# A transformer layer pair on eight cores: token-major residual, background stages behind both attentions

## The chip, the cores and the metric

The kernel runs on the 8 cores of one Trainium2 chip, in two dies of four cores. Every core computes one of the 8 batch elements alone; the cores exchange nothing. The metric is the device time of the slowest core, in microseconds (us).

## The reference, cut to what matters

One batch element is 2048 tokens of 1024 features. In sequence:

```python
x = x + attn_a(layernorm(x))   # 8 heads; two 64-wide halves q1,q2 / k1,k2 of each 128-wide head
x = x + ffn(layernorm(x))
x = x + attn_b(layernorm(x))   # 16 heads of 64, rotary, causal softmax
x = x + ffn(layernorm(x))      # the same ffn weights again
attn_a: # for each head, over all 2048 keys:
L1, L2 = cos_scale * l2norm(q1) @ l2norm(k1).T, cos_scale * l2norm(q2) @ l2norm(k2).T
G = tanh(delta_gain * (L1 - L2))
y = (softmax(L1 + G) - lambda * softmax(L2 - G)) @ v      # then an RMS norm over 128, @ Wo.T + bo
ffn: y = x @ int4_rounded(kernel) + bias + (x @ a) @ b    (a is 1024 x 16)
```

## The kernel before, in words

The residual stream is kept feature-major: `resid[c]` holds 128 features of all 2048 tokens (f32), eight such tiles. All stages follow one another, with a barrier of all engines (`phase_barrier`) between most of them:

1. Preparation: load the input, small constants; quantize the ffn weights on VectorE and ScalarE, 8 row blocks one after another, and store them in DRAM (`d_wqb`).
2. `emit_ln`: sums over features by matmuls with a column of ones (`ln_px`, `ln_pxq`), row arithmetic on one partition, a broadcast by matmul (`ln_bc`), two VectorE passes for each tile.
3. Attention A in two halves of four heads (`hg`). `run_qk_proj` makes Q and K; each group of 128 features and 512 tokens takes 8 matmuls, is squared, summed by head half with two one-column matmuls, and the norm goes through one-partition rows (`qrows`) with Ln and Exp on ScalarE. `emit_proj_tm` makes V.
4. The attention loop has 256 steps for each half, 512 in all; a step is 128 keys by 512 queries for both softmaxes. TensorE: a pair of logits (`a_pL<-aQ,aK`, each on 64 rows of the array), the scaled difference (`a_pD`), two additions of G by an identity and a negative identity (`id_bf`, `idn_bf`), two value products (`a_pY`) and two one-column sums (`a_ps`). ScalarE: one Tanh (`a_G<-a_pD`) and one Exp of 1024 columns (`a_E<-a_pL`). There are two buffers of each, and the order of an engine's instructions is written out by hand. The sums are turned into reciprocals by way of DRAM (`scr`, `xpf`, `scrb`, `a_rb`).
5. Output projection into `resid`, `emit_ln`, `emit_ffn`.
6. Layer norm, rotary tables, then two halves of attention B: projections with a swap matmul (`b_pswap`) and three VectorE passes for the rotation, then 160 steps of 128 keys by up to 512 queries for two heads: Exp (`b_E`), three value or sum matmuls, a mask on diagonal blocks.
7. Output projection, layer norm, ffn, and the store of all of `resid`.

Each instruction is recorded by a helper, so every row of the profile names line L119; the tile names tell them apart.

## Time and profile before

| | |
|---|---|
| median of 3 runs | 6092.5 us (6050.47 to 6096.83) |
| profiled execution, slowest core | span of 6033.8 us from first to last instruction |
| TensorE / VectorE / ScalarE / GpSimd busy | 2880.8 / 1456.7 / 1464.2 / 319.3 us |
| mean granted TensorE clock, die 0 / die 1 | 0.727 / 0.718 of full |
| moved by DMA | 83.52 MB, mean 14 GB/s |

The span is that of one profiled execution; the timed runs are 17 to 63 us above it. Busy time of TensorE counts the modelled time in the array, and matmuls overlap each other.

### The profile page before, as it was taken

How to read it: one execution, taken by the hardware profiler on the slowest of the kernel's cores; microseconds unless marked ns; L12 is line 12 of the kernel's file. 1: busy time of each engine (PE TensorE's matmuls, PEld its weight loads, DVE VectorE, ACT ScalarE, POOL GpSimd, SP SyncE). 2: the span in 40 equal slices, each digit the busy share in tenths (PEclk: the TensorE clock that was granted, in tenths of full speed). 3: DMA queues.
4: the chain of work that ended last, by engine and by line, in shares of the span. 5: the costliest groups of instructions: out<-in, count | busy, mean ns of one | idle time of the engine just before them, and what ended most of it. 6: DMA issues, size and time to landing. Idle time of an engine off the chain costs nothing.

```text
span 6033.8 us, 35983 instructions; the slowest of 8 cores (5950.4 to 6033.8 us)
## 1 busy us (share of the span) xinstructions
PE 2880.8 (48%) x9536; PEld 759.7 (13%) x9536; DVE 1456.7 (24%) x2432; ACT 1464.2 (24%) x1528; POOL 319.3 (5%) x535
## 2 busy tenths in 40 slices
PE   0012436666555443466556654352446544655625
PEld 0000111111111011111111111110111111111201
DVE  1335330000111133200100111515431225222241
ACT  0000113444444311144444441000003320233000
POOL 0100000000000000000000000000001100011000
PEclk9985556677777756777877686686776667766858
DMA  2000000000000000000000001000100000000101
GB/s 87 8 9 11 11 18 3 6 6 6 6 8 6 7 13 14 14 6 6 6 6 7 6 6 27 6 13 2 40 17 5 6 15 23 12 6 5 30 3 68
DMA packets 107520, 83.52 MB, mean 14 GB/s; under 512 B 45086, under 2 KB 94750, under 8 KB 105022
## 3 DMA queue, kind: packets, MB, share of 16 engines
q1 hardware_dynamic: 79710, 55.07, 3.0%
q0 software_dynamic: 27616, 26.14, 2.3%
q8 instruction: 87, 1.43, 0.1%
q14 instruction: 107, 0.88, 0.1%
HBM read 70.08 MB, written 10.98 MB: 13 GB/s over the span
## 4 chain that ended last, share of the span: by engine, by line
PE 34%; DVE 19%; DMA 19%; ACT 14%; issue 11%; DVEq 1%; ACTq 0%; POOLq 0%; SPq 0%; PEldq 0%; POOL 0%
ACT a_E L119 8%; PE pj_p L119 7%; PE a_pY L119 6%; PE a_pL L119 5%; DMA scrb<-xpb 4%; PE a_pD L119 3%; PE a_ps L119 3%; PE f_p L119 3%; DMA b_rb<-scrb 3%; DMA scr<-rr 3%; DVE tmpf L119 3%; PE tm_pv L119 2%; ACT qrows L119 2%; DMA wqb<-qout 2%; DMA xpf<-scr 2%
## 5 line engine op out<-in xcount | busy, mean ns | idle before, releaser
L119 PE MATMUL a_pY<-a_E,aV 128*128 128x512 bf16 x1024 | 393.0, 474 | 811.7 <-ACT a_E L119 811.6
L119 ACT ACTIVATE a_G<-a_pD,gvec 128x512 bf16<-128x512 f32 x512 | 352.7, 689 | 1197.2 <-PE a_pD L119 1188.7
L119 ACT ACTIVATE a_E<-a_pL,ccol 128x1024 bf16<-128x1024 f32 x512 | 569.6, 1112 | 94.0 <-PE a_pL L119 90.8
L119 ACT ACTIVATE b_E<-b_pS,ccol 128x1024 bf16<-128x1024 f32 (+1 forms) x320 | 312.3, 987 | 1121.3 <-PE b_pS L119 1119.3
L119 PE MATMUL b_pYa<-b_E,bV 128*65 128x512 bf16 (+1 forms) x320 | 145.0, 453 | 366.5 <-DVE b_E L119 262.4
L119 PE MATMUL ln_px<-ln_xb,ones_col 128*1 128x512 bf16 x128 | 74.4, 581 | 468.6 <-DVEq L119 468.6
L119 POOL DMA_DIRECT2D scr<-rr x160 | 81.3, 508 | 4023.2 <-DVEq L119 3914.5
L119 PE MATMUL a_pD<-aQ,aKn 128*128 128x512 bf16 x512 | 253.6, 495 | 44.4 <-DVEq L119 23.5
L119 ACT ACTIVATE qrows<-qrows 1x4096 bf16<-1x4096 bf16 x32 | 115.7, 3617 | 588.6 <-DVEq L119 587.1
L119 PE MATMUL a_pL<-a_G,id_bf 128*128 128x512 bf16 x512 | 257.9, 504 | 0.0
L119 PE MATMUL a_pL<-a_G,idn_bf 128*128 128x512 bf16 x512 | 253.7, 495 | 0.0
L119 PE MATMUL a_pL<-aQ,aK 64*128 64x512 bf16 x1024 | 252.0, 489 | 2.9 <-DVEq L119 2.9
L119 DVE COPY a_Yr<-a_pY 128x512 f32<-128x512 f32 x64 | 41.2, 686 | 862.0 <-PE a_ps L119 862.0
L119 PE MATMUL a_ps<-a_E,ones_col 128*1 128x512 bf16 x1024 | 242.8, 470 | 0.0
L119 PE MATMUL pj_p<-xnA,pj_wb 128*128 128x512 bf16 x512 | 203.0, 568 | 73.9 <-DVE pj_wb L119 73.9
L119 ACT ACT_TABLE_LOAD x69 | 88.5, 1283 | 540.4 <-DVEq L119 329.5
L119 PE MATMUL pj_p<-bxn,pj_wb 128*128 128x512 bf16 x512 | 154.4, 456 | 121.4 <-DVE pj_wb L119 121.4
L119 PEld LDWEIGHTS a_pY<-a_E,aV 128*128 128x128 bf16 x1024 | 67.2, 99 | 1143.9 <-issue 1143.9
L119 PE MATMUL f_p<-fxn,f_wqb 128*128 128x512 bf16 x512 | 149.5, 445 | 110.7 <-DVEq L119 57.1
L119 DVE RECIPROCAL xpb<-xpf 128x8 bf16<-128x8 f32 x96 | 18.7, 195 | 746.0 <-DMA xpf<-scr 484.4
L119 PE MATMUL pbcq<-qrows,ones_row 1*64 1x512 bf16 x128 | 40.5, 615 | 251.8 <-DVEq L119 251.8
L119 PE MATMUL b_pYb<-b_E,bV 128*64 128x512 bf16 (+1 forms) x320 | 150.1, 469 | 0.0
(151 smaller groups left out, 3170.0 us busy)
## 6 DMA issues: line engine op xcount, KB each, us to landing
a_rb<-scrb POOLq DMA_DIRECT2D x32, 256.0 KB, 3.9
pj_wf<-WqkT SPq DMA_DIRECT2D x32, 256.0 KB
out<-resid SPq DMA_DIRECT2D x8, 1024.0 KB, 10.2
resid<-xT SPq DMA_DIRECT2D x4, 1024.0 KB, 11.9
resid<-xT POOLq DMA_DIRECT2D x4, 1024.0 KB, 12.5
pj_wf<-WqT SPq DMA_DIRECT2D x16, 256.0 KB
pj_wf<-WkT SPq DMA_DIRECT2D x16, 256.0 KB
tm_wvhf<-WvT SPq DMA_DIRECT2D x16, 256.0 KB
```

Of the source, the lines that this page charges most:

```text
L119: r = getattr(eng, name)(*args, **kw)
```

## The change

The kernel is rewritten. In words, with the names of the new code:

- The residual is token-major: a block `b` is 128 tokens by 1024 features, 16 blocks, four of them at a time in `x`. Layer norm statistics come from `bn_stats` and `bn_aggr` on VectorE, the power -0.5 from GpSimd, and one VectorE pass applies them. Between the ffn and attention B the residual goes to DRAM (`d_x2`) and the normalized tokens too (`d_xn3`).
- The features are brought onto partitions by transposing DMAs on SyncE's queue (`Slot.turn`): of normalized blocks (`turn_ln1`, `turn_ln`, `load_xs`) and of attention outputs (`turn`, `turn_b`). Blocks 0 to 7 of the first layer norm are turned by 8 matmuls each with an identity (`turn_pe`), evicted by ScalarE and VectorE.
- Phase 1 makes Q, K and V of all heads: 64 groups for Q and K (8 matmuls and one with a block matrix `blk` that sums squares over a head half on all partitions; Square, Ln and Exp of 512 columns on ScalarE; one VectorE pass) and 32 for V. The weights are cast to bf16 by GpSimd's DMAs. The quantization (`quantize`) is a generator stepped between the groups and in phase 2; the result `wq` stays in SBUF.
- Phase 2 is attention A in 64 units (256 queries and one head) of 8 steps, 512 steps in all; a step is 256 keys by 256 queries. E is the stationary operand and V, with a column of ones, the moving one, so that outputs are token-major and the sums come with them: 8 matmuls of 129 columns. G is added on VectorE (`step_S`), on odd steps for the lower half by one matmul with a negative identity (`step_A`). The per-unit normalization is on GpSimd (`y_out`, `y_rms`).
- After 8 units a generator `after_a` does output projection, layer norm, ffn and the next layer norm of two blocks; `Background.step` puts up to 1.6 (later 3) matmuls of 512 columns of it into each attention step.
- Phase 3 makes K, V and Q of attention B for all heads (96 groups; GpSimd does the last addition of the rotation), phase 4 is attention B in 320 steps, with E stationary again (65 columns) and `after_b` in the background. The last four blocks' `after_b` runs after the loop.

The core of the diff (removed lines are those of the listing above):

```diff
+class Background:
...
+    def step(self, rate, cap):
+        self.clock += 1
+        due = [c for c in self.calls if c[0] <= self.clock]
+        self.calls = [c for c in self.calls if c[0] > self.clock]
+        for _, fn in due:
+            fn()
+        self.credit = min(self.credit + rate, cap)
+        while self.gens and self.credit > 0:
+            cost = next(self.gens[0], None)
+            if cost is None:
+                self.gens.popleft()
+                return
+            if cost <= 0:
+                return
+            self.credit -= cost
+    def drain(self):
...
+    def turn_pe(n):
+        for _ in range(n):
+            b, a_tok = late_turn.popleft()
+            t, tb = b // 4, b % 4
+            toks = []
+            pe.wait(a_tok)
+            for k, q in enumerate((ac, ve)):
+                pe.wait(pT_free[k])
+                for c in range(4):
+                    col = 128 * (4 * k + c)
+                    mm(pe, pT[k][:, 128 * c:128 * (c + 1)], wq[:, b % 8, col:col + 128],
+                       ident[:, :], True, True)
+                q.wait(pe.done())
+                out = xn[t % 2][:, 4 * k:4 * k + 4, 128 * tb:128 * (tb + 1)]
+                if q is ac:
+                    act(ac, out, blocks_of(pT[k][:, :], 4), AF.Copy)
+                else:
+                    copy(ve, out, blocks_of(pT[k][:, :], 4))
+                pT_free[k] = q.done()
...
+        ac.wait(p_tok, sq_free[i])
+        act(ac, sqb[i][:, :], bank[:, :], AF.Square)
+        sq_tok = ac.done()
+        def rest():
+            pe.wait(sq_tok, pss_free[i])
+            mm(pe, pss[i][:, :], blk[:, :], sqb[i][:, :], True, True)
+            s_tok = pe.done()
+            sq_free[i] = s_tok
+            ac.wait(s_tok, rn_free[i])
+            act(ac, rn[i][:, :], pss[i][:, :], AF.Ln, bias=lntiny)
+            pss_free[i] = ac.done()
+            ac.wait(pss_free[i])
+            if is_q:
+                act(ac, rn[i][:, :], rn[i][:, :], AF.Exp, scale=-0.5, bias=lnc[:, h:h + 1])
+            else:
+                act(ac, rn[i][:, :], rn[i][:, :], AF.Exp, scale=-0.5)
+            ve.wait(ac.done())
+            cap = c1e6[:, h:h + 1] if is_q else 1.0 / COS_EPS
+            stt(ve, dst[:, h, QT * t:QT * (t + 1)], rn[i][:, :], cap, bank[:, :], OP.min, OP.mult)
+            rn_free[i] = pqk_free[bi] = ve.done()
+        late.append(rest)
...
+        for t in (t0, t1):
+            for h in range(HA):
+                group_qk(Q, W3[0], w_tok[0:2], t, True, h)
+                if pair == 0 and t == t0:
+                    if h < 4:
+                        ln1_stats(4 + h)
+                    if 1 <= h < 5:
+                        ln1_apply(3 + h)
+                    if h >= 4:
+                        turn_pe(1)
+                if pair == 1:
+                    next(quant, None)
+        for t in (t0, t1):
+            for h in range(HA):
+                group_qk(K, W3[1], w_tok[2:4], t, False, h)
+                if pair == 0:
+                    (ln1_stats, ln1_apply)[h % 2](8 + 4 * (t - t0) + h // 2)
+                if pair == 1:
+                    next(quant, None)
+                if (pair == 0 and t == t1) or (pair == 1 and h % 2 == 1):
+                    next_v()
+        while todo_v:
+            next_v()
+    phase_barrier()
+    p1.close()
+    s1.close()
...
+        pe.wait(w_tok, *y_toks)
+        for hf in range(2):
+            cols = slice(512 * hf, 512 * (hf + 1))
+            bank = state["banks"].take(pe)
+            for c in range(NCH):
+                mm(pe, bank[0], Q[:, c, tok], Wo[:, c, cols], c == 0, c == NCH - 1 and not bias)
+                yield 1
+            if bias:
+                pe.wait(state["row97"])
+                mm(pe, bank[0], sel[:, :], fbb[:, cols], False, True)
+            p_tok = pe.done()
+            yield 0
+            ve.wait(p_tok, x_tok[b])
+            tt(ve, x[:, b % 4, cols], bank[0], x[:, b % 4, cols], OP.add)
+            bank[1] = ve.done()
+            yield 0
+            ve.wait(bank[1])
+            ln_stats(b, hf)
...
+        for hf in range(2):
+            cols = slice(512 * hf, 512 * (hf + 1))
+            bank = state["banks"].take(pe)
+            for c in range(NCH):
+                mm(pe, bank[0], xt[:, c, :], wq[:, c, cols], c == 0, False)
+                yield 1
+            pe.wait(l_tok)
+            mm(pe, bank[0], lora[k][:, :], fbb[:, cols], False, True)
+            p_tok = pe.done()
+            yield 0
+            ve.wait(p_tok)
+            stt(ve, x[:, b % 4, cols], bank[0], qscale[:, 0:1], x[:, b % 4, cols],
+                OP.mult, OP.add)
+            bank[1] = x_tok = ve.done()
+            yield 0
...
+    def after_a(n, y_toks):
+        last = n == NTB // 2 - 1
+        q = ve
+        two = (2 * n, 2 * n + 1)
+        if not last:
+            load_x(di["xN"], 2 * n + 2)
+            load_x(di["xN"], 2 * n + 3)
+        for i, b in enumerate(two):
+            yield from out_proj(b, y_toks, state["Wo"], True)
+            layer_norm(b, q, i, lambda a_tok, b=b, i=i: turn_ln(b, i, a_tok, b % 4))
+        if last:
+            state["last_o"](pe.done())
+        for i, b in enumerate(two):
+            yield from ffn(b, b % 4)
+            sy.wait(state["x"])
+            x2_tok[b] = r_st.next(sy).start(sy, rows_of(d_x2, b), x[:, b % 4, :])
+            layer_norm(b, q, 2 + i, lambda a_tok, b=b, i=i: keep(b, 2 + i, a_tok))
+        while xn3_tok[two[1]] is None:
+            yield 0
...
+    def on_pe(s):
+        return s % 2 == 1
+    def step_L(s):
+        if not 0 <= s < NS:
+            return
+        h, qsl = q_range(s // NKS)
+        pe.wait(S_tok.get(s - 2), P_tok.get(s - 2))
+        for jj in range(2):
+            j = 2 * (s % NKS) + jj
+            js = slice(128 * j, 128 * (j + 1))
+            cs = slice(QA * jj, QA * (jj + 1))
+            mm(pe, pL[2 * (s % 2)][:, cs], K[0:64, h, js], Q[0:64, h, qsl], True, True, (0, 0))
+            if on_pe(s):
+                pe.add(lambda e, s=s, cs=cs, js=js, h=h, qsl=qsl, jj=jj: e.matmul(
+                    pL[2 * (s % 2) + 1][:, cs], K[64:128, h, js], Q[64:128, h, qsl],
+                    start=jj == 0, stop=False, tile_position=(64, 0), skip_group_check=True))
+            else:
+                mm(pe, pL[2 * (s % 2) + 1][:, cs], K[64:128, h, js], Q[64:128, h, qsl], True, True,
+                   (64, 0))
+        L_tok[s] = pe.done()
+    def step_A(s):
+        if not 0 <= s < NS or not on_pe(s):
+            return
+        pe.wait(G_tok[s])
+        mm_in(pe, pL[2 * (s % 2) + 1][:, :], nident[:, :], Gt[s % G_RING][:, :], False, True)
+        A_tok[s] = pe.done()
+    def step_D(s):
+        if not 0 <= s < NS:
+            return
+        u = s // NKS
+        h, _ = q_range(u)
+        pe.wait(G_tok.get(s - 1), qn_tok[u])
+        for jj in range(2):
+            j = 2 * (s % NKS) + jj
+            mm(pe, pD[:, QA * jj:QA * (jj + 1)], K[:, h, 128 * j:128 * (j + 1)], Qn[u % 2][:, :],
+               True, True)
+        D_tok[s] = pe.done()
+    def step_tanh(s):
+        if not 0 <= s < NS:
+            return
+        ac.wait(D_tok[s], S_tok.get(s - G_RING), A_tok.get(s - G_RING))
+        act(ac, Gt[s % G_RING][:, :], pD[:, :], AF.Tanh)
+        G_tok[s] = ac.done()
+    def step_S(s):
+        if not 0 <= s < NS:
+            return
+        ve.wait(L_tok[s], G_tok[s], E_tok.get(s - S_RING))
+        sx, gt = Sx[s % S_RING], Gt[s % G_RING]
+        tt(ve, sx[:, 0, :], pL[2 * (s % 2)][:, :], gt[:, :], OP.add)
+        if not on_pe(s):
+            tt(ve, sx[:, 1, :], pL[2 * (s % 2) + 1][:, :], gt[:, :], OP.subtract)
+        S_tok[s] = ve.done()
+    def step_exp(s):
+        if not 0 <= s < NS:
+            return
+        e = E[s % E_RING]
+        ac.wait(Y_tok.get(s - E_RING))
+        if on_pe(s):
+            ac.wait(A_tok[s])
+            act(ac, e[:, 1, :, :], pL[2 * (s % 2) + 1][:, :], AF.Exp)
+            P_tok[s] = ac.done()
+            ac.wait(S_tok[s])
+            act(ac, e[:, 0, :, :], Sx[s % S_RING][:, 0, :], AF.Exp)
+        else:
+            ac.wait(S_tok[s])
+            act(ac, e[:, :, :, :], Sx[s % S_RING][:, :, :], AF.Exp)
+        E_tok[s] = ac.done()
+    def step_Y(s):
+        if not 0 <= s < NS:
+            return
+        u, k = s // NKS, s % NKS
+        h, _ = q_range(u)
+        pe.wait(E_tok[s])
+        if k == 0:
+            pe.wait(y_evac.get(u - 1))
+        for jj in range(2):
+            for sg in range(2):
+                for b in range(2):
+                    mm_in(pe, pY[sg][:, VA * b:VA * (b + 1)],
+                          E[s % E_RING][:, sg, jj, 128 * b:128 * (b + 1)],
+                       V[:, 2 * k + jj, VA * h:VA * (h + 1)],
+                       k == 0 and jj == 0 and b == 0, k == NKS - 1 and jj == 1)
+        Y_tok[s] = pe.done()
...
+    for s in range(-3, NS + NKS):
+        step_tanh(s + 2)
+        step_exp(s)
+        u, k = (s - NKS) // NKS, s % NKS
+        if u < 0 or k == 0 or k >= 3:
+            step_Y(s - 1)
+        elif k == 2:
+            step_Y(s - 2)
+            step_Y(s - 1)
+        step_D(s + 3)
+        step_L(s + 2)
+        step_A(s + 1)
+        if u >= 0 and k == 1:
+            y_out(u, 1)
+        step_S(s + 1)
+        if s >= 0:
+            bg.step(1.6, 2.6)
+        if u >= 0:
+            if k == 0:
+                y_out(u, 0)
+            if k == 4:
+                y_rms(u)
+            if k == 6:
+                turn(u)
+        if s >= 0 and k == 5:
+            make_qn(s // NKS + 2)
...
+    def load_xs(t, *free):
+        sy.wait(*xn3_tok[4 * t:4 * t + 4], *free)
+        xs_tok[t] = r_turn.next(sy).turn(sy, xs[t], rows_of(d_xn3, t, QT))
...
+        ac.wait(p_tok, qb_free[i])
+        act(ac, qb[i][:, :], bank[:, :], AF.Copy)
+        b_tok = ac.done()
+        def rest():
+            pe.wait(b_tok, pss_free[i])
+            mm(pe, pss[i][:, :], perm[:, :], qb[i][:, :], True, True)
+            qb_free[i] = pe.done()
+            ve.wait(b_tok, t_free[i], cs_tok[t])
+            tt(ve, t1[i][:, :], bank[:, :], x[:, t, 0:QT], OP.mult)
+            pqk_free[bi] = ve.done()
+            ve.wait(qb_free[i])
+            tt(ve, t2[i][:, :], pss[i][:, :], x[:, t, QT:2 * QT], OP.mult)
+            pss_free[i] = ve.done()
+            po.wait(pss_free[i])
+            tt(po, dst[:, h, sl], t1[i][:, :], t2[i][:, :], OP.add)
+            t_free[i] = po.done()
...
+    def after_b(t, y_toks):
+        four = range(4 * t, 4 * t + 4)
+        for b in four:
+            yield from out_proj(b, y_toks, wo_tok, False)
+            layer_norm(b, ve, b % 4, lambda a_tok, b=b: turn_ln(b, b % 4, a_tok, b % 4))
+        for b in four:
+            yield from ffn(b, b % 4)
+            sy.wait(state["x"])
+            out_tok[b] = x_free[b % 4] = r_st.next(sy).start(sy, rows_of(d_out, b), x[:, b % 4, :])
+            if b + 4 < NTB:
+                load_x(d_x2, b + 4)
...
+        pe.wait(E_tok.get(s - 2))
+        mm(pe, pS[s % 2][:, 0, q0:QT], K[0:64, c, js], Q[0:64, c, qsl], True, True, (0, 0))
+        mm(pe, pS[s % 2][:, 1, q0:QT], K[64:128, c, js], Q[64:128, c, qsl], True, True, (64, 0))
+        S_tok[s] = pe.done()
...
+    for s in range(-2, NB + 5):
+        stepb_exp(s)
+        stepb_Y(s - 2)
+        if 0 <= s - 2 < NB:
+            t, c, j = blocks[s - 2]
+            if j == 4 * t + 3:
+                i = t * (HB // 2) + c
+                k = norm_b(t, c, i, s - 2)
+                turn_b(t, c, i, k)
+        if s >= 0:
+            bg.step(3, 3)
+        stepb_S(s + 2)
+    for k in range(4):
+        state["banks"].add(pS[k // 2][:, k % 2, :], E_tok[NB - 1])
+    bg.drain()
```

## Rows read from the trace of the kernel before

**Rows 1.** Cores: span and mean granted clock, slowest core and both dies.
```profile
core 7: 6033.8 us, clock 0.718
die 0 (median of its cores): 5976.8 us, clock 0.727
```

**Rows 2.** Windows by stage: us, busy (count) of each engine, clock, DMA.
```profile
0.00:380.00 380.00, 0.00 (x0) 0.00 (x0) 98.36 (x154) 20.09 (x21) 44.90 (x87) 1.00 0.13 39
380.00:922.00 542.00, 204.58 (x584) 61.06 (x584) 223.57 (x300) 64.56 (x25) 0.00 (x0) 0.58 0.04 12
922.00:2040.00 1118.00, 683.45 (x2255) 141.47 (x2256) 107.56 (x194) 483.16 (x545) 78.49 (x135) 0.73 0.03 6
2040.00:2540.00 500.00, 194.25 (x621) 58.45 (x621) 154.00 (x210) 81.75 (x43) 5.23 (x9) 0.62 0.05 14
2540.00:3700.00 1160.00, 664.75 (x2276) 141.17 (x2276) 114.76 (x207) 484.84 (x550) 83.16 (x143) 0.75 0.05 6
3700.00:4478.00 778.00, 334.50 (x1138) 116.36 (x1138) 331.31 (x497) 12.10 (x17) 0.54 (x1) 0.73 0.07 20
4478.00:5630.00 1152.00, 610.00 (x2016) 175.99 (x2016) 294.02 (x680) 312.31 (x320) 107.02 (x160) 0.67 0.04 10
5630.00:6034.00 404.00, 189.26 (x648) 65.21 (x648) 133.15 (x190) 5.41 (x8) 0.00 (x0) 0.74 0.11 36
```

**Rows 3.** Chain that ended last, one step of attention A: start, us, what.
```profile
1499.91 0.59 PE a_pY L119 x2
1500.50 0.31 PE a_ps L119 x2
1500.81 0.32 PE a_pL L119 x2
...
1501.61 0.33 ACT a_G L119
...
1502.19 1.12 ACT a_E L119
...
1503.44 0.59 PE a_pY L119 x2
```

**Rows 4.** Costliest groups: shapes, count, busy, mean ns, idle before.
```profile
L119 ACT ACTIVATE a_E<-a_pL,ccol 128x1024 bf16<-128x1024 f32 x512 | 569.6, 1112 | 94.0 <-PE a_pL L119 90.8
L119 ACT ACTIVATE a_G<-a_pD,gvec 128x512 bf16<-128x512 f32 x512 | 352.7, 689 | 1197.2 <-PE a_pD L119 1188.7 <-PE a_pL L119 8.5
L119 PEld LDWEIGHTS a_pY<-a_E,aV 128*128 128x128 bf16 x1024 | 67.2, 99 | 1143.9 <-issue 1143.9
L119 DVE SCALAR_TENSOR_TENSOR resid<-f_p,fb_col,resid 128x512 f32<-128x512 f32 x64 | 48.0, 751 | 233.9 <-PE f_p L119 233.9
L119 DVE TENSOR_TENSOR aQ<-aQ,pbcq 128x512 bf16<-128x512 bf16 x32 | 22.0, 688 | 35.2 <-PE pbcq L119 35.2
```

**Rows 5.** Timeline of ScalarE: two Exp of 1024 columns back to back.
```profile
4495.88 2.15 ACT L119 ACTIVATE b_E<-b_pS,ccol 128x1024 bf16<-128x1024 f32 x2 [0.85 <-PE b_pS L119]
```

**Rows 6.** Timeline of weight loads in a dense run of 512-column matmuls.
```profile
3751.35 4.63 PEld L119 LDWEIGHTS pj_p<-aQ,pj_wb 128*128 128x128 bf16 x22 [0.20 <-issue]
```

**Rows 7.** Window of core 7 in its first dense V projection.
```profile
900.00:910.00 10.00, 10.00 (x40) 4.15 (x39) 3.46 (x5) 0.00 (x0) 0.00 (x0) 0.81 0.00 0
```

**Rows 8.** The same window on core 0.
```profile
900.00:910.00 10.00, 10.00 (x48) 4.55 (x47) 4.15 (x6) 0.00 (x0) 0.00 (x0) 1.00 0.01 2
```

**Rows 9.** Timeline of core 7's weight loads there, first and thirty-second.
```profile
900.24 0.11 PEld L119 LDWEIGHTS tm_pv<-tm_wvh,xnA 128*128 128x128 bf16 x1 [0.15 <-issue]
...
908.38 0.11 PEld L119 LDWEIGHTS tm_pv<-tm_wvh,xnA 128*128 128x128 bf16 x1 [0.15 <-issue]
```

**Rows 10.** DMA queue: packets, MB, share; issues: count, KB, us to landing.
```profile
q1 hardware_dynamic: 79710, 55.07, 3.0%
...
a_rb<-scrb POOLq DMA_DIRECT2D x32, 256.0 KB, 3.9
...
out<-resid SPq DMA_DIRECT2D x8, 1024.0 KB, 10.2
```

2008 lines of the change are left out of this document (857 added, 1151 removed).

## The prediction

> **What bounds the kernel now.** I read the cores first: the slowest spans 6033.8 us, the other die's median is within 1% of it, so one core tells the story [rows 1]. Then windows cut by stage [rows 2]. The reader should see that no engine is full anywhere: in attention A (1118 + 1160 us) TensorE is busy 61% and 57% and ScalarE 43% and 42%; outside the attentions ScalarE does almost nothing and TensorE 25 to 45%; in the first 380 us TensorE does nothing at all. The stages stand in a row, so the kernel is bound by waits, and each stage's latency counts in full. The chain of waits shows the same inside a step of attention A [rows 3]: value products, sums, logits, then Tanh, then Exp, then the next value products, 1503.44 - 1499.91 = 3.53 us a step where it runs at its best, of which ScalarE works 1.8 and TensorE about 2. Over the halves it is (1118 + 1160)/512 = 4.45 us, since the idle lets the granted clock drop to 0.73 [rows 2].
>
> **Prices.** Dense 512-column matmuls start 0.215 us apart at a granted clock of 1.0 (4.63 us for 22 loads, less one load of 0.11) [rows 6]. In the dense V projection core 7 was granted 0.81 for all of the window, its TensorE busy without a gap [rows 7], and starts were (908.38 - 900.24)/31 = 0.263 us apart [rows 9]; core 0 kept 1.00 in the same work [rows 8]. A pair on 64 rows each runs together, 0.32 us for both [rows 3]. Exp of 1024 columns takes 1.11 us, back to back 2.15 - 1.11 = 1.04 [rows 4, 5]; Tanh of 512 takes 0.69, and Exp starts 0.58 after it [rows 3, 4]. VectorE takes 0.69 for 512 columns with a PSUM input, 0.75 with three operands [rows 4]. No row has a 129- or 65-column matmul that loads new weights each time. Below, it cannot beat a quarter of 0.215, 0.054; above, a whole weight load of 0.099 [rows 4] that nothing hides. I take 0.075, since loads are pulled ahead of the running matmul in every dense row, but a 129-column one is too short to hide one fully.
>
> **The clock decides the sum.** The new kernel keeps TensorE dense nearly throughout, on all cores at once. The only stretch here like that is rows 7, and it ran at 0.81 on the slower die. I take 0.81 for TensorE-bound stages. The Trainium skill (TensorE: Matmul & The Clock Gate, Part 1) states that dense matmuls on three or more cores of a die bring that die to 13/16 of the clock for as long as the load lasts. By that rule, the trace agrees on core 7 (0.81) and not on core 0 (1.00); under the rule both dies would drop, and the sum would be the one I take.
>
> **Part by part, removed against added.**
> 1. *Preparation*, 380 us [rows 2]. Quantization moves between projection groups and behind attention A: 24 VectorE passes of 1024 columns plus reductions, hidden because VectorE otherwise has one or two 0.7 us passes in each 2.3 us group; without that cover some 40 us. What stays is filling: four 512 KB token blocks and 2 MB of the first weights (1 MB lands in 10.2 us when eight are in flight [rows 10]), then statistics, GpSimd power, apply and turn. 25 us exposed, bounds 15 and 50.
> 2. *First norm, Q, K, V*, 542 + 500 = 1042 us [rows 2], becomes 64 x 9 + 32 x 8 = 832 matmuls: 832 x 0.263 = 219 us (179 at full clock). ScalarE has Square, Ln, Exp in each Q or K group: 0.58 + 0.69 + 0.58 and about 0.2 of waits (Exp waits for its own engine's Ln) = 2.05, under TensorE's 9 x 0.263 = 2.37, but over 1.94 at full clock. 222 us; 190 at full clock.
> 3. *Attention A*, 2278 us. TensorE in a step: 8 x 0.075 = 0.60; logits 2 pairs of 256 columns, 0.32; difference 0.22; half an addition 0.11; background 14 blocks x (36 x 0.215 + 0.5) = 115 us / 512 = 0.22. Sum 1.47, or 1.47/0.81 = 1.81. ScalarE: even steps 0.58 + 1.04, odd steps 3 x 0.58, mean 1.68. VectorE: 1.5 passes of 0.69 = 1.03, background and eviction 0.35: 1.4, not last. The engines are in order, and one wait is new: there is one difference bank, so `step_D` stands behind the Tanh of the same iteration, and logits, addition and background are queued behind it. TensorE's iteration is then 0.79 (Tanh and its signal; the value products fit in it) + (0.22 + 0.32 + 0.11 + up to 0.35 background) = 1.8 at full clock and 0.79 + 1.23 = 2.02 at 0.81. Taking 2.05: 512 x 2.05 = 1050 us (1.85: 947). With 0.054 or 0.099 for the small matmul the value products stay between 0.43 and 0.98, so only the upper end reaches past the 0.79: 0.2 x 512 = 100 us more. Plus 15 us to fill, load the identity and a ScalarE table.
> 4. *Output projection, norms, ffn of A*, 340 of the 778 us: behind attention, priced above. Each step's matmuls go between `step_A` and the next value products, so they delay the latter on TensorE; that is the 0.35. Exposed: 5 us at the end, and the last two blocks, in part 5.
> 5. *Projections of B*, the other 438 plus the 260 inside the B window: again 832 matmuls, 219 us (179). In each group ScalarE has one copy, VectorE two passes (1.4), GpSimd one 512-column addition; all under 2.37 if GpSimd's is. Before it 1 MB has to be transposed after the last value product: 12 us [rows 10]. The last two blocks' background, 74 matmuls = 19 us, and its norms, of which 20 stay exposed. 270 us (221).
> 6. *Attention B*, 892 us without the projections. Full steps: TensorE 0.32 + 8 x 0.075 = 0.92, ScalarE 1.04; diagonal ones about 0.6 and 0.75. Without background ScalarE leads: 0.97 on average. Twelve blocks of background are 12 x 12 = 144 steps with three more matmuls: (0.87 + 0.65)/0.81 = 1.85. 32 first steps 27 us, 144 x 1.85 = 266, 144 x 1.08 = 156: 449 us (387). Start-up 10.
> 7. *Output of B*, 404 us: three quarters hidden; the last four blocks are 4 x 36 x 0.263 = 38 us, plus a norm, a transpose and the last store, 20 us. 58 us (50).
>
> Sum: 25 + 222 + 1050 + 15 + 5 + 270 + 459 + 58 = **2104 us** of span, against 6034. The timed runs before are 17 to 63 us over the span, the median 59; that gives a median near **2140 us**. At full clock throughout: 25 + 190 + 947 + 15 + 5 + 221 + 397 + 50 = 1850, median 1890.
>
> **GpSimd and the transposes** have no row of their own. GpSimd gets five 256-column passes and some ten tiny ones in each unit of 8 steps (16 us), and one 512-column pass in each rotation group. Below zero is excluded, as it frees nothing that is last; it costs nothing up to about 2.5 us for a 256-column pass and 2.3 us for the 512-column one. The nearest row, VectorE's 0.69 for 512 [rows 4], leaves a factor of three. I take nothing. The Trainium skill (GPSIMD Engine Reference, 3.1) speaks against this part of the change: it calls GpSimd the wrong place for ordinary elementwise work, about twice VectorE's time; no run here shows it yet, and an estimate from its 4497 ns for 2048 columns is 1.1 to 1.3 us for the rotation's addition, still hidden.
>
> **Rivals.**
> *A: the clock stays at 1.0* on the slowest core as core 0's did [rows 8]: 1890 us. For it: one die shows it. Against it: the slowest core counts, and there are far longer dense stretches. 0.25.
> *B: the in-order chain of attention does not close.* Each engine of a step waits for two others, plus VectorE's background passes ahead of `step_S`. If each step of A loses another 0.4 us and each of B 0.2: 205 + 64 = 270 us, 2400 us. For it: before, a step whose parts sum to about 2 us took 3.53 [rows 3]. Against it: three or four buffers now instead of two, and logits issued two steps ahead. 0.20.
> *C: slower than before, through the transposing DMAs.* They carry 8 blocks of the first norm and 2048 x 1024 elements five more times (outputs of A, second norm, third norm, outputs of B, last norm): 11.5 million 2-byte elements. The hardware queue's packets took 0.030 x 16 x 6033.8 / 79710 = 36 ns each [rows 10]. If a transpose moved each element as a packet, 11.5 million x 36 ns / 16 engines = 26 ms. It decides from 5.4 ns an element, where 11.5 million x 5.4 / 16 makes up the 3900 us gained; that is 5.9 GB/s. Against it: a rewrite of whole blocks needs no such packets, and at the rate of plain copies (1 MB in 10 us) each transpose is hidden. The Trainium skill (DMA: Bandwidth & Descriptors, latency table) gives 261 GB/s for one transposing kernel; no run here shows it. 0.02. A milder form, transposes at a tenth of plain rate, would add some 100 us at the ends of phases and lies in the range.
> *The change does not do what it says*: no time is hidden, as the background waits at the head of its queue. The hidden parts (115 + 100 us of matmuls) would come back, twice with waits: 2350; counted with B.
>
> **How the numbers follow.** Forecast 2140 us, 0.53; A 0.25; B 0.20; C 0.02. The range 1870 to 2430 takes in A with the cheap matmul, and B; the bounds of filling and of the 0.099 matmul lie within. A measurement of this kernel tells about 1% from no change. Faster by over 1%: all but C, 0.975; within 1%: 0.005, a C that lands there; slower 0.02.
>
> **What would show it.** Granted clock 0.81 in the dense phases on core 7 or its like; attention A's period near 2.05 us with ScalarE busy over 85% and the matmuls of `step_D` waiting for Tanh; first matmul of a group before 30 us; B's projections about 2.4 us a group; after the attention B loop some 60 us. The prediction is wrong if the period of A is over 2.4 us, if a transpose takes over 10 us to land, if GpSimd is busy over 80% in attention A, or if the gaps between the phases sum to over 80 us.

## The result, and the profile after

| | before | after |
|---|---|---|
| median | 6067.23 us (6034.74 to 6096.83, 5 runs) | 1807.96 us (1740.35 to 1873.85, 5 runs) |
| span of the profiled execution | [rows 1] | 1738.1 us (time 1740.44) |

The ratio is **0.2868**, 95% interval 0.2848 to 0.2889. Three of the five runs after (1807.96, 1824.82, 1873.85) had the cores of one die or of both at a lower mean clock (0.84 to 0.91 against 0.95 to 0.96), in the same program, so the ratio and every comparison below leave such runs out, while medians and ranges count all runs.

The forecast was 2140 us, range 1870 to 2430. It was wrong: median and profiled execution both lie below the range. The side was that of rival A, the full clock, which was priced at 1890 us; at 1740 us the kernel is 8% below even that.

The slowest core of the changed kernel, span and mean granted clock, answers to [rows 1]; the medians of the two dies are 1734.9 and 1733.3 us, both at 0.957:

```profile
core 2: 1738.1 us, clock 0.957
```

Its stages in windows, columns as in [rows 2]: filling; first norm and projections of A; attention A, cut in four; projections of B; attention B; what is left.

```profile
0.00:34.70 34.70, 4.22 (x33) 3.06 (x34) 11.93 (x28) 4.95 (x6) 12.68 (x22) 1.00 0.87 179
34.70:241.40 206.70, 188.36 (x866) 84.05 (x866) 112.66 (x188) 123.91 (x203) 15.70 (x35) 0.97 0.35 74
...
241.40:450.00 208.60, 186.11 (x1907) 104.99 (x1908) 170.23 (x287) 191.93 (x315) 89.59 (x191) 0.96 0.23 61
450.00:650.00 200.00, 190.82 (x1979) 108.56 (x1978) 162.81 (x285) 191.94 (x313) 95.10 (x217) 1.00 0.13 36
650.00:850.00 200.00, 190.41 (x1980) 108.47 (x1977) 162.12 (x285) 191.35 (x312) 96.29 (x221) 1.00 0.13 38
850.00:1070.00 220.00, 208.86 (x2173) 119.09 (x2172) 179.62 (x313) 211.07 (x343) 104.87 (x240) 1.00 0.14 38
...
1070.30:1326.70 256.40, 203.39 (x927) 90.42 (x926) 98.20 (x157) 57.32 (x96) 96.95 (x98) 0.90 0.32 55
1326.70:1693.40 366.70, 319.17 (x3319) 151.88 (x3320) 127.07 (x360) 296.20 (x320) 16.15 (x51) 0.91 0.28 67
1693.40:1738.00 44.60, 35.13 (x170) 15.25 (x170) 22.20 (x40) 0.00 (x0) 5.85 (x16) 0.92 0.26 74
```

The reader should see two things. In attention A TensorE is busy 95% and ScalarE 96% of each window from 450 us on (89 and 92% in the first), where [rows 2] had 61 and 43% in the first half: two engines are nearly full at once. And the clock column reads 1.00 from 450 to 1070 us, with TensorE busy 95%; the other seven cores show 1.00 there too, at 92 to 95%. The term on which the sum was built, 0.81, is not there. Nor is it in the projections of A, which are the same kind of work as [rows 7]: from 100 to 230 us all eight cores have TensorE busy 98 to 100% at 1.00, here the slowest core:

```profile
100.00:230.00 130.00, 128.27 (x594) 57.62 (x593) 72.44 (x110) 74.43 (x120) 3.96 (x10) 1.00 0.22 56
```

The groups of attention A, columns as in [rows 4]:

```profile
L175 ACT ACTIVATE Gt<-pD 128x512 bf16<-128x512 f32 x512 | 306.5, 599 | 25.4 <-PE pD L164 16.5
L171 PE MATMUL pY<-V,E 128*128 128x129 bf16 x4096 | 308.5, 221 | 11.7 <-ACT E L175 2.6
L164 PE MATMUL pD<-Qn,K 128*128 128x256 bf16 x1024 | 196.2, 273 | 21.0 <-ACT Gt L175 12.7
```

The difference matmuls waited for Tanh (`Gt`) 12.7 us in the whole run, not the better part of every step. Two steps of the loop on TensorE and on ScalarE (start, us, what):

```profile
601.08 0.62 PE L171 MATMUL pY<-V,E 128*128 128x129 bf16 x8
601.53 0.38 PE L164 MATMUL pD<-Qn,K 128*128 128x256 bf16 x2
...
602.17 0.39 PE L164 MATMUL pB<-Wo,Q 128*128 128x512 bf16 x1
602.40 0.62 PE L171 MATMUL pY<-V,E 128*128 128x129 bf16 x8
602.86 0.38 PE L164 MATMUL pD<-Qn,K 128*128 128x256 bf16 x2
603.17 0.39 PE L166 MATMUL pL<-Q,K 64*128 64x256 bf16 x4
603.50 0.39 PE L171 MATMUL pL<-Gt,nident 128*128 128x512 bf16 x1
603.72 0.59 PE L164 MATMUL pB<-Wo,Q 128*128 128x512 bf16 x2
604.15 0.34 PE L171 MATMUL pY<-V,E 128*128 128x129 bf16 x3
```

```profile
601.48 0.63 ACT L175 ACTIVATE E<-Sx 128x512 bf16<-128x512 f32 x1
602.01 0.60 ACT L175 ACTIVATE Gt<-pD 128x512 bf16<-128x512 f32 x1
602.51 1.05 ACT L175 ACTIVATE E<-Sx 128x1024 bf16<-128x1024 f32 x1
603.46 0.59 ACT L175 ACTIVATE Gt<-pD 128x512 bf16<-128x512 f32 x1
603.98 0.60 ACT L175 ACTIVATE E<-pL 128x512 bf16<-128x512 f32 x1
```

TensorE's busy time counts the modelled time in the array, so starts give the better prices. Eight value matmuls take 601.53 - 601.08 = 0.45 us, 0.056 each, though each loads new weights. ScalarE starts something 0.50 to 0.53 us after an operation of 512 columns and 0.95 after one of 1024. An iteration takes 602.40 - 601.08 = 1.32 with one background product (`pB`), 604.15 - 602.40 = 1.75 with an addition and two of them; the mean is 829/512 = 1.62. Between 300 and 1060 us the median from the last difference matmul to the logits is 0.20 us and from the logits to an addition or a background product 0.20 too, against 0.11 between two difference matmuls of the same 256 columns. An estimate from these starts: 0.45 + 0.11 + 0.20 + 0.12 + 0.20, half an addition (0.11) and a background product (0.22) are 1.41 of the 1.62 us, so TensorE is taken for 87% of the loop rather than 95.

At the seam between attention A and the projections of B, and in the first 80 us of the latter, TensorE and SP's queue (start, us, what, idle before):

```profile
1069.95 0.62 PE L171 MATMUL pY<-V,E 128*128 128x129 bf16 x8 [0.38 <-ACT E L175]
1080.95 1.44 PE L164 MATMUL pB<-Wo,Q 128*128 128x512 bf16 x3 [10.38 <-DMA Q<-yt]
1093.00 3.24 PE L164 MATMUL pL<-V,wkb 128*128 128x512 bf16 x8 [10.61 <-DMA V<-xn]
1115.79 3.57 PE L164 MATMUL pL<-V,wkb 128*128 128x512 bf16 x8 [10.48 <-DMA V<-xn]
1150.37 1.01 PE L164 MATMUL pB<-xn,fab 128*16 128x128 bf16 x8 [16.99 <-DMA xn<-xn]
```

```profile
1078.47 1.17 SPq L127 DMA_TRANSPOSE Q<-yt  x1
1079.79 7.63 SPq L127 DMA_TRANSPOSE V<-xn  x1
...
1088.76 23.49 SPq L127 DMA_TRANSPOSE V<-xn  x1
1135.25 2.81 SPq L127 DMA_TRANSPOSE xn<-xn  x1
```

The first K product waits for a 1 MB transpose that stands on the queue behind the last small one, which itself waits for GpSimd's norm of the last rows. The longest of the four waits, 17.0 us, is for a transpose of 256 KB (`xn<-xn`) that the background's last ffn needs: it landed 15.0 us after its issue, with two weight loads of 1 MB (`Wo<-WqB`) under way, where such a transpose takes 3.1 us in the median of the whole run.

### The profile page after: what moved, and what is told of

It reads as the page before. It is cut to its first block, busy times and chain, and to the rows that moved or that the text cites. A ratio compares the mean times of both kernels' runs of the same rounds, so it can differ in the third digit from the quotient of the medians.

```text
span 1738.1 us, 40419 instructions; the slowest of 8 cores (1726.8 to 1738.1 us)
## 1 busy us (share of the span) xinstructions
PE 1526.8 (88%) x13344; PEld 786.1 (45%) x13344; DVE 1046.8 (60%) x1939; ACT 1268.7 (73%) x1904; POOL 533.2 (31%) x1089
## 3 DMA queue, kind: packets, MB, share of 16 engines
q1 hardware_dynamic: 113718, 82.10, 17.8%
q8 instruction: 115, 1.88, 0.4%
## 4 chain that ended last, share of the span: by engine, by line
PE 43%; ACT 22%; issue 11%; DVE 4%; DMA 4%; POOL 1%; SPq 1%; ACTq 0%; DVEq 0%; POOLq 0%
ACT E L175 11%; PE pL L164 9%; PE pY L171 7%; ACT Gt L175 7%; PE pBb L164 6%; PE pB L164 4%; PE pL L166 4%; PE pS L166 4%; PE pYb L171 4%; ACT EB L175 4%; PE pD L164 3%; DMA V<-xn 2%; DVE Sx L184 1%; DMA Q<-ytb 1%; PE pS L164 1%
## 5 line engine op out<-in xcount | busy, mean ns | idle before, releaser
L184 DVE TENSOR_TENSOR Sx<-pL,Gt 128x512 f32<-128x512 f32 x768 | 503.3, 685 | 139.9 <-PE pL L955 53.3
L175 ACT ACTIVATE E<-Sx 128x1024 bf16<-128x1024 f32 (+1 forms) x512 | 433.1, 846 | 16.5 <-DVE Sx L184 16.1
L175 ACT ACTIVATE EB<-pS,cst 128x1024 bf16<-128x1024 f32 (+1 forms) x320 | 296.2, 992 | 73.1 <-PE pS L166 67.5
L175 ACT ACTIVATE Gt<-pD 128x512 bf16<-128x512 f32 x512 | 306.5, 599 | 25.4 <-PE pD L164 16.5
L171 PE MATMUL pY<-V,E 128*128 128x129 bf16 x4096 | 308.5, 221 | 11.7 <-ACT E L175 2.6
L171 PEld LDWEIGHTS pY<-V,E 128*128 128x128 bf16 x4096 | 259.9, 98 | 93.6 <-issue 41.9
L166 PE MATMUL pL<-Q,K 64*128 64x256 bf16 x1536 | 198.7, 274 | 24.0 <-ACT E L175 15.7
L164 PE MATMUL pD<-Qn,K 128*128 128x256 bf16 x1024 | 196.2, 273 | 21.0 <-ACT Gt L175 12.7
L175 ACT ACTIVATE E<-pL 128x512 bf16<-128x512 f32 x256 | 154.1, 602 | 6.0 <-PE pL L171 0.9
L171 PE MATMUL pYb<-V,EB 128*128 128x65 bf16 x2176 | 132.5, 200 | 10.3 <-DVE EB L184 5.5
L955 PE MATMUL pL<-Q,K 64*128 64x256 bf16 x512 | 100.2, 276 | 0.0
```

The costliest lines, as they stand in the source:

```text
L164: q.add(lambda e: e.matmul(out, lhsT, rhs, start=start, stop=stop))
L166: q.add(lambda e: e.matmul(out, lhsT, rhs, start=start, stop=stop, tile_position=pos))
L171: q.add(lambda e: e.matmul(out, lhsT, rhs, start=first, stop=last, skip_group_check=True))
L175: q.add(lambda e: e.activation(out, in_, func, **kw))
L184: q.add(lambda e: e.tensor_tensor(out, a, b, op))
L955: pe.add(lambda e, s=s, cs=cs, js=js, h=h, qsl=qsl, jj=jj: e.matmul(pL[2 * (s % 2) + 1][:, cs], K[64:128, h, js], Q[64:128, h, qsl], start ...
```

## The experiments

The first six take attention A apart; its length is from the first Tanh to the last value product, 829 us in the changed kernel (241.4 to 1070.3). Two theories stood against each other: its period is ScalarE's, or it is TensorE's.

**1. A per-partition bias on every Tanh and Exp of A** (adds to ScalarE alone).
```diff
+    memset(ve, zerob, 0.0)
-        act(ac, Gt[s % G_RING][:, :], pD[:, :], AF.Tanh)
+        act(ac, Gt[s % G_RING][:, :], pD[:, :], AF.Tanh, bias=zerob)
# and the same on the three Exp of A
```


> Tanh and the Exps of attention A get a zero column as bias, so ScalarE does the same work with one more operand. Before, Tanh with such an operand took 0.689 us, here without it 0.597; I expect 0.06 to 0.09 us on each of the 2.5 instructions of a step. Theory S (ScalarE sets the period of attention A, 1.625 us): the period grows by 0.15 to 0.22, attention A (832 us) by 75 to 115 us, the span from 1738 to 1815-1850. Theory T (TensorE's in-order queue behind the one difference bank sets it): attention A grows by under 25 us.

**2. Every difference matmul issued twice** (adds to TensorE alone).
```diff
-            mm(pe, pD[:, QA * jj:QA * (jj + 1)], K[:, h, 128 * j:128 * (j + 1)], Qn[u % 2][:, :],
-               True, True)
+            for _ in range(2):
+                mm(pe, pD[:, QA * jj:QA * (jj + 1)], K[:, h, 128 * j:128 * (j + 1)],
+                   Qn[u % 2][:, :], True, True)
```


> Both difference matmuls of each step are done twice into the same bank: 2 x 0.108 = 0.215 us more for TensorE in each step, right behind the wait for Tanh. Theory T: the period grows by all of it, attention A by 110 us, span about 1848. Theory S: TensorE has slack of about 0.2 us a step, attention A grows by under 40 us, span under 1780.

**3. No background in attention A** (the same work runs after the loop).
```diff
-            bg.step(1.6, 2.6)
+            pass
```


> No background in attention A's loop: all of it (quantization's rest, ffn preparation, output projection, norm, ffn of 14 more blocks) runs after the loop. Theory S: the period falls only to what ScalarE issues, about 1.48 us, attention A to 760-790 us. Theory T: TensorE loses 0.22 us a step, attention A falls by 110 us to about 720. What follows the loop grows by 14 blocks at 12 to 18 us, 170 to 250 us: span about 1890 to 1950. That is the value of hiding this work.

**4. As 3, with a second bank for the difference** (the part of the matmul's output memory that it is written to): `step_D` waits for the Tanh of two steps before, not of one.
```diff
-        pe.wait(G_tok.get(s - 1), qn_tok[u])
+        pe.wait(G_tok.get(s - 2), qn_tok[u])
-            mm(pe, pD[:, QA * jj:QA * (jj + 1)], ...
+            mm(pe, (pD, pB)[s % 2][:, QA * jj:QA * (jj + 1)], ...
# Tanh reads the same bank, and bg.step is left out as in 3
```


> As e3_nobg_a, and the background's bank serves as a second bank for the difference, so the difference matmuls wait for the Tanh of one step earlier. Theory T (the gate of my prediction): attention A falls by more than 40 us against e3. Theory S: within 15 us of e3.

| | median, us | ratio to before | span | attention A |
|---|---|---|---|---|
| 1 bias | 1802.77 (1802.73 to 1802.81, 2 runs) | 0.2965 [0.2935, 0.2994] | 1801.1 | 887, +58 |
| 2 twice | 1887.54 (1811.74 to 1983.73, 4) | 0.2981 [0.2951, 0.3010] | 1812.0 | 896, +67 |
| 3 no background | 2039.87 (2012.58 to 2067.16, 2) | none given | 2011.0 | 764.6, -64 |
| 4 and two banks | 2086.98 (2009.64 to 2098.58, 3) | none given | 2008.1 | 763.2, -66 |

Attention A as a window, first of run 1:

```profile
245.30:1132.20 886.90, 810.21 (x8038) 446.49 (x8038) 680.49 (x1167) 873.87 (x1280) 382.74 (x867) 0.99 0.15 41
```

of run 2:

```profile
246.70:1142.70 896.00, 870.62 (x9059) 539.45 (x9060) 681.05 (x1167) 808.98 (x1280) 383.08 (x867) 0.99 0.15 40
```

of run 3:

```profile
243.90:1008.50 764.60, 652.45 (x7294) 393.49 (x7422) 567.18 (x957) 758.36 (x1280) 345.57 (x755) 0.99 0.05 9
```

and of run 4:

```profile
247.20:1010.40 763.20, 665.60 (x7422) 387.89 (x7420) 567.59 (x957) 758.50 (x1280) 345.45 (x755) 1.00 0.04 9
```

Run 1: the 1280 operations became 0.11 us longer each (Tanh 0.599 to 0.706 us, Exp of 1024 columns 1.061 to 1.171), some 138 us in all (an estimate from the means), and 58 came through, 42%. Run 2: 1024 matmuls of 256 columns at 0.1075 are 110 us, and 67 came through, 61%; Tanh's waits for the difference grew from 16 to 57 us between 241 and 1000 us. So neither theory holds alone.

The starts of Tanh in the traces tell why. Here the steps are sorted, two at a time, by how many background products started in them; the numbers are the median length of one step in us.

| background products in two steps | none | one | three (run 1: four) | five |
|---|---|---|---|---|
| changed kernel | 1.45 | 1.49 | 1.53 | 1.70 |
| 1 bias | 1.68 | 1.68 | 1.68 | 1.72 |
| 2 twice | 1.54 | 1.60 | 1.76 | 1.92 |

In steps without background the bias, 2.5 x 0.11 = 0.27 us of ScalarE a step, shows as 0.23, and the doubled difference, 0.22 of TensorE, as 0.09. With five products the bias shows as 0.02 and the doubled difference in full, as 0.22. Each step is thus mostly one engine's: ScalarE's where little background stands in it, TensorE's where there is much. The 42 and 61% are averages over both kinds.

Runs 3 and 4 give the floors. Without background ScalarE is busy 758 of 765 us, 99%: that is its floor, 1.48 us a step. TensorE's busy time falls from 776 to 666 (run 4; run 3's trace lacks 128 matmul records), so the background is 111 us of it, 0.22 a step. Run 4 takes away the wait for Tanh and gains nothing over run 3: in run 3 the difference matmuls waited 47.4 us for Tanh, in run 4 not at all, and the logits waited 55.5 us for Exp instead (10.9 in run 3). That gate does not bound the loop there. With background in the loop it was not tried, since `pB` serves the background; the 12.7 us of waiting above bound it.

Run 3 also prices the hiding. The loop gets 64 us shorter and the kernel 2011.0 - 1738.1 = 273 longer, so what hid in attention A takes 273 + 64 = 337 us when it stands alone (170 to 250 was expected), and costs 64 inside. The first 291.5 us after the loop show TensorE busy 130 us at a clock of 0.77:

```profile
1008.50:1300.00 291.50, 130.26 (x520) 50.81 (x528) 112.61 (x183) 0.00 (x0) 34.18 (x103) 0.77 0.27 87
```

**5 and 6. The lower gate addition always on VectorE, or always on TensorE** (the change alternates them).
```diff
-        return s % 2 == 1
+        return False        # 5; in 6: return True
```


> All gate additions on VectorE (no matmul with the negative identity, Exp always of 1024 columns). VectorE then has 2 x 0.69 = 1.37 us in every step and 0.35 of background and eviction, 1.7 us against the period of 1.62. I expect VectorE to set the period at about 1.73: attention A 880 to 900 us, span 1790 to 1810. If only ScalarE and TensorE mattered, attention A would fall by 10 to 30 us, as both lose work.

> The lower gate addition on TensorE in every step. TensorE +0.11 us a step, ScalarE +0.03, VectorE -0.34. If steps with background work are TensorE-bound and the others ScalarE-bound (as e1 to e4 read), attention A grows by about 0.6 x 0.11 x 512 = 34 plus 6 us: span about 1775. If VectorE counted in the present mix, it would not grow.

5 took 1760.62 us (1759.88 to 1761.36, 2 runs), ratio 0.2864 [0.2833, 0.2894], attention A 846.6 us, +18; 6 took 1790.96 (1789.77 to 1792.15, 2), ratio 0.2913 [0.2881, 0.2945], attention A 877.5, +49. The windows of 5 and, below it, of 6:

```profile
245.00:1091.60 846.60, 736.83 (x7782) 414.17 (x7782) 806.14 (x1423) 759.98 (x1024) 383.24 (x867) 0.98 0.15 42
```

```profile
243.10:1120.60 877.50, 827.54 (x8294) 472.37 (x8294) 530.77 (x911) 827.28 (x1536) 384.63 (x867) 0.99 0.15 41
```

In 5 VectorE becomes the full engine, 806 of 847 us (95%), and between 241 and 1000 us ScalarE's Exp waits 62.5 us for it, against 15.1. Still the loop came out 33 to 53 us shorter than was expected. In 6 VectorE falls to 60%, and TensorE and ScalarE both get more to do (256 more additions; two Exp of 512 in place of one of 1024). The alternation keeps VectorE at 81%, TensorE at 94 and ScalarE at 95.

These verdicts rest on the loop's length and the windows. The intervals of the whole-kernel ratios of 5, 6 and 7 overlap that of the change, and the kernel before took 6122 to 6163 us beside runs 5 to 8, against 6035 to 6104 beside the change and runs 1 to 4, so that ratios of this group come out lower. Attention A repeats better: 828 to 830 us in all seven profiled executions whose edit leaves it alone (the changed kernel twice, and 7 to 11).

**7. The first eight token blocks turned by DMA instead of by TensorE.**
```diff
-    turn_pe(4)
+    turn_ln1(4)
-                        turn_pe(1)
+                        turn_ln1(1)
```


> The first eight token blocks are turned by transposing DMAs instead of matmuls. The DMA engines are 95% busy in the first 50 us, so the four first transposes come late: the first projection matmul at 40 to 50 us instead of 34.7, span +5 to +20 us. Rival: a transpose lands in 3 us as in attention A and the span stays within 5 us.

1774.52 us (1773.27 to 1775.77, 2 runs), ratio 0.2886 [0.2855, 0.2918], span 1774.1: 36 us longer, more than was expected. The first projection matmul and what SP's queue did:

```profile
29.71 27.10 SPq L127 DMA_TRANSPOSE xn<-wq  x4
```

```profile
67.86 2.72 PE L164 MATMUL pqk<-xn,w_q 128*128 128x512 bf16 x6 [67.86 <-DMA xn<-wq]
```

Four transposes of 256 KB held the queue for 27 us while the weights were still arriving, and the first product came at 67.9 instead of 34.7: 33 of the 36 us stand there. Inside attention A TensorE waits for a transpose 0.9 us in all.

**8. No bias in attention B's Exp.** The constant shift of -4 is left out; it is the same in numerator and denominator of the softmax.
```diff
-        act(ac, e[:, :, q0:QT], pS[s % 2][:, :, q0:QT], AF.Exp, scale=0.125, bias=shiftb)
+        act(ac, e[:, :, q0:QT], pS[s % 2][:, :, q0:QT], AF.Exp, scale=0.125)
```


> The Exp of attention B without its shift of -4 as a bias column (the shift cancels in the softmax). e1 priced such an operand at 0.10 us an instruction, 320 x 0.10 = 32 us of ScalarE. If attention B (368 us) is ScalarE-bound in all steps, span -32; if it is mixed like A, -12 to -20; if TensorE-bound, 0.

1732.13 us (1731.83 to 1732.44, 2 runs), ratio 0.2817 [0.2788, 0.2847], span 1730.1. The group, against `296.2, 992` in the changed kernel:

```profile
L175 ACT ACTIVATE EB<-pS 128x1024 bf16<-128x1024 f32 (+1 forms) x320 | 271.2, 906 | 86.3 <-PE pS L166 80.3 <-PE pYb L171 3.4
```

ScalarE works 25 us less, the stretch of value products in B shrank by 11 (358.8 to 347.5), the span by 8 (12 to 20 was expected of a mixed bound), and ScalarE's waits for the logits grew by 13 (67.5 to 80.3). That attention B too is shared between the two engines is read from this, not tested by adding to TensorE.

The ratios of the last four, the changed kernel itself among them, are to 7 runs of the kernel before (6085.35 us, 6047.34 to 6192.96).

**9. Token loads first, K and V weights after the first norm.**
```diff
-    load_x1(0)
-    load_x1(1)
+    for b in range(4):
+        load_x1(b)
-    load_x1(2)             # behind the eight small loads
-    load_x1(3)
+    load_w3(1, "WkT")      # behind the first turn
+    load_w3(2, "WvT")
```


> The loads of the first four token blocks go ahead of the eight small constant loads on SyncE's queue, and the K and V weights are loaded only after the first four blocks' norm. If the fill is bound by these loads (blocks 2 and 3 landed at 22.6 and 25 us behind the constants and 12 MB of weights), the first projection matmul starts at 22 to 27 us instead of 34.7 and the span falls by 8 to 12 us. If it is bound by the DMA engines' total work (95% busy), it falls by under 3 us, or the K weights come late and it grows.

**10. First 1 MB transpose of B's input ahead of the last small one, K products by token tile.**
```diff
+        if s == NS + 2:
+            turn_xs(0, Y_tok[NS - 1])
-        for hf in range(2):
-            for t in two:
-                for h in range(4 * hf, 4 * hf + 4):
+        for t in two:
+            for h in range(HA):
```


> The first 512-token transpose of phase 3 is issued ahead of the last unit's own transpose, and K's groups take all heads of one token tile before the next, so the second transpose has four more groups to land in. After: the first K matmul came 23 us after attention A's last value product and TensorE waited 10.5 us more for the second tile. I expect 8 and 8 to 10 us less: span -12 to -18 us.

**11. Edits 8, 9 and 10 together, and the triangular mask loaded during B's projections** (its load had held the first diagonal block of B for 9.3 us).
```diff
+            tri_tok = sl_c[0].start(po, sel[:, :], di["tri"])
-    ve.wait(sl_c[2].start(po, tri[:, :], di["tri"]))
+    ve.wait(tri_tok)
```


> e8, e9 and e10 together, and the causal mask loaded in phase 3 instead of at the start of phase 4, where VectorE waited until 7 us after the first Exp. Sum of the parts: -8 (e8) -10 -15 -6: span near 1700 us, 2% under the changed kernel. If the parts share a bound (the DMA engines), under half of it.

**12. The changed kernel again.**

> The changed kernel itself on this chip, to compare the others with: span 1738 within 10 us, and in which share of its runs a die is granted less clock.

| | median, us | ratio to before | span | first product | attention A from | first K product of B |
|---|---|---|---|---|---|---|
| 9 | 1734.33 (1733.87 to 1734.8, 2 runs) | 0.2855 [0.2839, 0.2871] | 1733.1 | 28.6 | 234.4 | |
| 10 | 1768.05 (1737.25 to 1791.74, 3) | none given | 1734.7 | | | 1084.1 |
| 11 | 1711.53 (1710.13 to 1853.38, 4) | 0.2818 [0.2802, 0.2833] | 1707.1 | 23.4 | 233.8 | |
| 12 | 1744.01 (1741.91 to 1902.61, 4) | 0.2870 [0.2858, 0.2882] | 1741.6 | 34.0 | 244.3 | 1096.5 |

The stages of 11 from the end of attention A on (up to the first value product of B; from there to the last):

```profile
1061.80:1314.60 252.80, 205.76 (x916) 91.51 (x931) 98.67 (x159) 59.38 (x99) 99.00 (x101) 0.90 0.36 57
1314.60:1662.80 348.20, 310.37 (x3269) 150.23 (x3312) 126.48 (x359) 269.35 (x318) 14.13 (x48) 0.93 0.29 70
```

and of 12:

```profile
1073.80:1338.40 264.60, 204.99 (x932) 90.86 (x930) 98.69 (x160) 60.23 (x100) 99.31 (x101) 0.89 0.33 59
1338.40:1696.80 358.40, 319.31 (x3312) 151.98 (x3312) 126.62 (x359) 293.45 (x316) 13.65 (x48) 0.91 0.26 64
```

11 is 34.5 us shorter than the changed kernel by the spans, 2.0%, where 39 were expected, and its interval lies below 12's: it is the fastest version found by its time. (The ratio of 8 is as low, 0.2817, but to a kernel before that took 6122 to 6163 us.) The gain is 10.6 us in filling, 1.5 in attention A (829.5 to 828.0), 11.8 up to B's first value product (B's input and the mask), 10.2 from there on. 9 alone moves the start of attention A by 10 us; its first product, at 28.6, came a little later than the 22 to 27 expected.

10 alone gave 7 us where 12 to 18 were expected. The K product came 12 earlier, but its trace shows where the wait went:

```profile
1116.25 3.57 PE L164 MATMUL pL<-V,wkb 128*128 128x512 bf16 x8 [20.46 <-DMA wkb<-WkB]
```

With all heads of a token tile first, the second half of the K weights (`wkb`) is needed after four groups instead of eight, and beside the second 1 MB transpose it landed 33 us after its issue, against 17 in the changed kernel. TensorE's waits in this stage are 10.4, 20.5 and 14.4 us, 45 in all, against 48 in 12. In 11 the same wait for the weights is 13.5 us. By whole times, 9 and 10 are not told from no change.

## Why the prediction was wrong

**The step that failed is "I take 0.81 for TensorE-bound stages".** It put 2104 - 1850 = 254 us on the span. It rested on 10 us of one core [rows 7] against the same 10 us of another [rows 8], and the longer dense stretches were taken to make the lower clock certain. They did not: in the profiled execution 130 us of projections with TensorE 98 to 100% busy, and 620 us of attention A with TensorE 92 to 95% busy, were granted 1.00 on all eight cores. Two background products start 0.59 - 0.38 = 0.21 us apart there, the full-clock price of [rows 6]. The Trainium skill (TensorE: Matmul & The Clock Gate, Part 1) states 13/16 for as long as three cores of a die run dense matmuls; by that rule, the profiled execution does not agree. What decides which clock is granted is left open: no experiment touched it. The honest use of rows 7 and 8 would have been two cases of like weight. Rival A had the clock right, at a chance of 0.25.

**The clock alone does not explain the miss.** At full clock the forecast was 1890 us, and 1740 was measured. Of these 150 us, 112 are in the sum of the terms, and the term that failed there is attention A's period of 1.85 us, measured at 1.62 (below). The other 38 are the step from span to time. The prediction added 36 to 40 us because the timed runs before stood 17 to 63 us over the span, but those were other executions: in every recorded one the time is 1.5 to 3.0 us over the span of its own slowest core (1740.44 against 1738.1).

**Against the full-clock sum of 1850 us**, term by term, as measured in the profiled execution (the windows above; they sum to 1738). Two slips of the sum are small: the parts of B's projections at full clock add to 227 us, not 221, and 1.52/0.81 is 1.88, not 1.85.

| | forecast | measured | |
|---|---|---|---|
| filling | 25 | 34.7 | +10 |
| first norm, Q, K, V | 190 | 206.7 | +17 |
| attention A and its start | 962 | 828.9 | -133 |
| end of the background, projections of B | 226 | 256.4 | +30 |
| attention B | 397 | 366.7 | -30 |
| rest | 50 | 44.6 | -5 |

*Attention A.* The second step that failed is the formula of 0.79 us for Tanh and its signal plus 0.22 + 0.32 + 0.11 + up to 0.35 for what is queued behind it. Tanh waits for `step_D` alone, so logits, addition and background run beside it; the gate closes D, Tanh, D, about 0.2 + 0.6 us and signals, under TensorE's own 1.3 to 1.75. Run 4 and the 12.7 us of waiting show it. The two loads that stood beside the formula were nearer: TensorE's 1.47 a step at full clock against the 1.41 counted above, and ScalarE's 1.68, which alone would have given 512 x 1.68 = 860 us against 829. In both a price was too high. The value matmul of 129 columns takes 0.056, near the lower bound of 0.054, not 0.075; eight a step make 0.15 us. And ScalarE's interval was read from [rows 4], where Tanh and Exp each have a per-partition operand (`gvec`, `ccol`), which the changed ones have not: a start every 0.50 to 0.53 us, and 0.95 for 1024 columns, not 0.58 and 1.04. Its floor is 1.48 (run 3), and run 1 puts 0.11 on such an operand. The Trainium skill (ScalarE: Activation LUTs, What ACT_TABLE_LOAD costs) states about 93 ns for each, and that operations one behind the other overlap by as much; run 1 measured 107 to 110 ns, and the starts above overlap by 0.07 to 0.10 us. Rival B's stalls did not come: a step takes 0.14 us more than ScalarE's floor on average, not 0.4 over 2.05.

*Background.* 115 us of TensorE, 0.22 a step, was forecast; run 4 gives 111. Right.

*Filling.* The sum of 25 left out the eight small constant loads on SP's queue ahead of the third and fourth token block, and that the three first weight matrices share the DMA engines with them. Experiment 9 takes 5 to 6 of the 10 us back; in 11 the first product came at 23.4. Turning on TensorE was priced at nothing beside DMA; experiment 7 puts 33 us on it at the first product, and so the forecast's argument that at the rate of plain copies each transpose is hidden is wrong for the first blocks.

*First norm and projections.* 1.94 us a group for TensorE at full clock and 2.05 for ScalarE was the right pair; TensorE was busy 188 of 207 us, and 8.2 of the rest is its wait at the end for GpSimd's first `Qn`, which the forecast had counted in the 15 us to start attention A. The other 10 were not taken apart.

*Projections of B.* The 12 us for 1 MB transposed were taken from a plain copy [rows 10] and were right for the first one, which landed after 13, but it is one wait of four that stand in series: 10.4, 10.6, 10.5 and 17.0 us, 48 in all, while the forecast exposed 12 + 20. The second transpose held the queue for 23 us. The clock falls with the waits; the first window holds the first two of them, the second the longest:

```profile
1070.00:1093.00 23.00, 2.01 (x11) 0.71 (x12) 1.18 (x3) 0.00 (x0) 8.37 (x15) 0.54 0.64 94
...
1130.00:1150.00 20.00, 3.39 (x16) 1.36 (x14) 5.57 (x10) 1.19 (x2) 6.92 (x9) 0.67 0.81 108
```

TensorE had 2.0 and 3.4 us of work there, and the granted clock was mostly its lower level, 1.2 GHz. Experiment 10 brings the first K product 12 us forward and keeps 7 of them, since the next wait grows.

*Attention B.* 30 us too high in all, with the same price for the small matmul; its terms were not read apart. Inside the 367 us lie 11 for the bias of its Exp (experiment 8) and 8 until the first value product, most of it the wait for the mask.

*GpSimd* at nothing: right inside the loops as far as shown. It was busy 386 of 829 us in attention A (47%, where the forecast named 80 as its limit), and took 1.27 us for the 512-column addition where 1.1 to 1.3 was estimated. At both ends it is in the chain: attention A starts behind its `Qn` (8.2 us), and at the seam its norm of the last rows takes 6.7 of the 10.4 us.

*Rival B* is refuted by A's period, 1.62 us against 2.05 + 0.4. *Rival C*: no transpose is near an element a packet; the hardware queue moved 113718 packets in the whole run, for 11.5 million elements transposed, and the largest two transposes landed after 13 and 27 us. By "a transpose takes over 10 us to land" the forecast named itself wrong there, and the place it did harm was the seam, as the mild form had it. *That the change does not do what it says*: run 3 shows 273 us of hiding. Of the signs named, ScalarE over 85% in attention A came (95%); the period of 2.05, the wait for Tanh and a first group before 30 us did not; a group of B's projections took 1.94 us where nothing was waited for, not 2.4, and after attention B 45 us were left, not 60.

## What to carry to other kernels

A price is read from a row with the same operands, not only the same shape: one per-partition operand was a sixth of a Tanh. Where a clock has two values in the trace, carry both cases to the end and weigh them, and do not let the longer load decide. Before laying a wait on a period, write down what the waiting engine has queued between cause and wait: what runs beside the wait is not added to it. In a loop where two engines are nearly full, ask which steps are whose: of what was added to one engine its own steps showed 0.23 of 0.27 us and all of 0.22, the other's 0.02 and 0.09, and the average over the loop, 42 and 61% here, says neither. And when an input is brought forward, look for the next one that the same work waits for.
